# Cross-partition maxima of the activation quantisers: the first over TensorE, GpSimd's last elementwise step given to ScalarE, a rearranged chain of constants, and three output pieces for the first batch

## What is computed

```python
def act_qdq(x, bits=16):
    qmax = 2 ** bits - 1
    mn = jnp.minimum(jnp.min(x), 0.0)          # over the whole tensor
    mx = jnp.maximum(jnp.max(x), 0.0)
    scale = jnp.maximum((mx - mn) / qmax, 1e-12)
    zp = jnp.clip(jnp.round(-mn / scale), 0, qmax)
    q = jnp.clip(jnp.round(x / scale) + zp, 0, qmax)
    return (q - zp) * scale

x = x + xattn(layernorm(x), ctx, Wq, Wk, Wv, Wo)
h = act_qdq(layernorm(x))                       # quantiser 1
up, gate = act_qdq(h @ wu.T), act_qdq(h @ wg.T) # quantisers 3 (up) and 2 (gate)
sig = fixed_qdq(sigmoid(gate), 1 / 65536)
p = act_qdq(gate * sig)                         # quantiser 3 (product)
o = act_qdq(p * up)                             # quantiser 4
x = x + o @ wd.T
```

## Time and profile before

| | |
|---|---|
| executions shown | 863.89, 864.57, 865.39 us |
| profiled execution, own time | 863.88 us |
| its span, first to last instruction | 862.1 us |
| mean granted TensorE clock | 0.966 of full speed |
| busy: TensorE / VectorE / ScalarE / GpSimd | 782.7 / 628.7 / 454.9 / 250.8 us |

### The profile page before, as it was taken

How to read it: one execution, slowest core, us unless ns; L and a number is a source line. 1 busy time by engine, 2 the same in 40 slices (tenths; PEclk the granted TensorE clock), 3 DMA queues, 4 the chain that set the end, 5 groups by cost and what they waited for, 6 DMA issues and landing times. The chain is left out here.

```text
span 862.1 us, 12646 instructions
## 1 busy us (share of the span) xinstructions
PE 782.7 (91%) x4746; PEld 465.3 (54%) x4746; DVE 628.7 (73%) x1141; ACT 454.9 (53%) x965; POOL 250.8 (29%) x382
## 2 busy tenths in 40 slices
PE   8998899999999999999999999997879999600998
PEld 3455466666666666666666666654334444200443
DVE  5873577788768778777788779986475489899741
ACT  5253456656556655566556555555140089495730
POOL 0210314356433466334455443442000012112000
PEclk9999999999999999999999999999989999955999
DMA  9121146756455575456664566997440000000000
GB/s 324 55 81 42 49 122 145 159 127 145 98 131 143 144 171 123 92 141 159 141 151 104 120 137 133 168 169 129 79 81 0 1 1 1 0 1 0 25 37 36
DMA packets 203437, 85.50 MB, mean 99 GB/s; under 512 B 170352, under 2 KB 186736, under 8 KB 203376
## 3 DMA queue, kind: packets, MB, share of 16 engines
q1 hardware_dynamic: 203376, 84.69, 43.1%
HBM read 31.72 MB, written 10.75 MB: 49 GB/s over the span
## 5 line engine op out<-in xcount | busy, mean ns | idle before, releaser
L314 PE MATMUL bank<-arena 128*128 128x256 f16 (+1 forms) x1872 | 261.0, 292 | 5.2 <-DVE arena L729 3.8
L314 PEld LDWEIGHTS bank<-arena 128*128 128x128 f16 x1872 | 182.8, 98 | 87.4 <-DVE arena L729 5.7
L1101 POOL TENSOR_SCALAR arena<-arena,rsum 128x256 f32<-128x256 f32 x256 | 133.7, 522 | 311.3 <-DVE rsum L793 297.3
L729 DVE SCALAR_TENSOR_TENSOR arena<-bank,arena 128x512 f16<-128x512 f32 x168 | 114.7, 688 | 118.1 <-ACT arena L541 117.7
L541 ACT ACTIVATE arena<-bank 128x512 f16<-128x512 f32 x168 | 98.7, 598 | 169.5 <-PE bank L414 93.9
L729 DVE SCALAR_TENSOR_TENSOR arena<-arena 128x512 f16<-128x512 f32 (+3 forms) x195 | 171.2, 889 | 15.3 <-ACT arena L541 14.7
L541 ACT ACTIVATE arena<-arena 128x512 f16<-128x512 f32 (+4 forms) x171 | 135.5, 813 | 61.7 <-POOL arena L1101 19.3
L583 ACT ACTIVATE arena<-bank,nmax 128x256 f32<-128x256 f32 x256 | 117.8, 472 | 60.0 <-DVE nmax L785 58.4
L428 PE MATMUL bank<-arena 128*128 128x512 f16 x512 | 122.4, 382 | 1.7 <-ACT arena L541 1.6
L484 PE MATMUL bank<-arena 128*128 128x512 f16 x528 | 116.7, 385 | 5.8 <-DVE arena L729 5.8
L404 PE MATMUL bank<-arena 128*128 128x256 f16 x768 | 94.3, 273 | 2.8 <-DVE arena L729 2.8
(11 more groups left out here) (87 smaller groups left out, 572.3 us busy)
## 6 DMA issues: line engine op xcount, KB each, us to landing
arena<-in_w_units SPq DMA_DIRECT2D x33, 256.0 KB, 3.6
w_ready<-arena SPq DMA_DIRECT2D x33, 256.0 KB, 3.3
arena<-in_wq SPq DMA_DIRECT2D x32, 256.0 KB, 3.5
arena<-in_wo SPq DMA_DIRECT2D x32, 256.0 KB, 3.6
arena<-in_x SPq DMA_DIRECT2D x1, 2048.0 KB, 15.1
out<-arena SPq DMA_DIRECT2D x8, 256.0 KB, 2.0
arena<-in_wk SPq DMA_DIRECT2D x4, 256.0 KB, 4.0
arena<-in_ctx_t SPq DMA_DIRECT2D x4, 256.0 KB, 4.6
```

The source lines that it names most:

```text
L314: last = nc.tensor.matmul(bank, a(i, c), b(j, c), start=start and c == 0 and n == 0, stop=stop and c == chunks - 1 and n == 2)
L729: return nc.vector.scalar_tensor_tensor(out=dst, in0=src, scalar=scale, in1=part, op0=ALU.mult, op1=ALU.subtract)
L1101: done = nc.gpsimd.tensor_scalar(p_s[:, t % 2, :, hh, :], p_s[:, t % 2, :, hh, :], rsum[:, t % 2, hh:hh + 1], P_SCALE, ALU.mult, ALU.mult)
```

## The change

1. A new path for quantiser 1. After `transpose_x2(B - 1)` TensorE waits for `worst_out` 1 and transposes the 128x2 worst values to 2x128 in PSUM. VectorE takes the maximum of the two rows, spreads it on a 2x2 diagonal, TensorE multiplies that by a 2x128 matrix of ones, which puts both values on all 128 partitions, and VectorE copies them. `all_reduce(1)` is gone, and 14 products on zeros become 12, after this.
2. The last of GpSimd's 11 sigmoid steps (L1174) goes to ScalarE, behind its own L696.
3. The clamp at zero moves out of the chain: `stats` gets one more column, which is zero and takes part in the reductions. The chain to `q_inv` has four steps instead of five, and the one from `q_inv` to `q_set` has one more.
4. Batch 0 of the final rounding goes in three pieces (tiles 0 to 1, 2 to 4, 5 to 10) instead of two.

```diff
-OQ_AT = (0, 5, FT)
+OQ_PIECES = [(0, 0, 2), (0, 2, 5), (0, 5, FT)] + [(b, *span) for b in range(1, B) for span in ((0, 5), (5, FT))]
...
+        ones = f32(178, P)
...
-        stats = small("stats", [P, 5, 2, 2 * FT])
+        stats = small("stats", [P, 5, 2, 2 * FT + 1])
+        x_worst = small("x_worst", [P, 4])
...
             transpose_x2(B - 1)
-            keep_warm(14)
+
+            pe.wait_ge(worst_out, 1)
+            nc.tensor.transpose(banks[SC][0:2, 0:P], worst[:, 0, :], ident[:, :]).then_inc(x_turned, 1)
+            pe.wait_ge(ones_set, 1)
+            pe.wait_ge(x_diag, 1)
+            nc.tensor.matmul(banks[SC + 1][:, 0:2], ones[0:2, :], x_worst[0:2, 1:3], start=True, stop=True).then_inc(x_spread, 1)
+            keep_warm(12)
...
+                    if z == FT - 1:
+                        act.wait_ge(sig_left, FT)
+                        nc.scalar.activation(sig[:, s, :], sig[:, s, :], ACT.Copy, bias=-QMAX, scale=1.0).then_inc(sig_end, 1)
...
             nc.vector.memset(mhalf[:, :], -0.5).then_inc(mhalf_set, 1)
+            nc.vector.memset(stats[:, :, :, :], 0.0).then_inc(stats_set, 1)
+            dve.wait_ge(stats_set, 1)
...
+            nc.vector.memset(ones, 1.0).then_inc(ones_set, 1)
             add_y(STEPS - 1)
...
                 red.then_inc(worst_out, 1)
-                dve.wait_ge(worst_red, number)
-                sets = [(qc[:, q, :], worst_all[:, i, :], worth) for i, (q, _, worth) in enumerate(tensors)]
-                for c, w, worth in sets:
-                    op = nc.vector.tensor_scalar(c[:, 0:2], w, 0.0, worth, ALU.max, ALU.mult)
+                if number == 1:
+                    dve.wait_ge(x_turned, 1)
+                    nc.vector.tensor_reduce(x_worst[0:2, 0:1], banks[SC][0:2, 0:P], AX.X, ALU.max).then_inc(x_top, 1)
+                    dve.wait_ge(x_top, 1)
+                    nc.vector.tensor_scalar(x_worst[0:2, 1:3], ident[0:2, 0:2], x_worst[0:2, 0:1], None, ALU.mult).then_inc(x_diag, 1)
+                    dve.wait_ge(x_spread, 1)
+                    chain(nc.vector.tensor_copy(worst_all[:, 0, :], banks[SC + 1][:, 0:2]))
+                else:
+                    dve.wait_ge(worst_red, number - 1)
+                sets = [(qc[:, q, :], worst_all[:, i, :], worth, -1.0 if q == QP else 1.0) for i, (q, _, worth) in enumerate(tensors)]
+                for c, w, worth, sign in sets:
+                    op = nc.vector.tensor_scalar(c[:, 2:3], w[:, 0:1], w[:, 1:2], 1.0 / QMAX, ALU.add, ALU.mult)
                 chain(op)
-                for c, w, worth in sets:
-                    op = nc.vector.tensor_tensor(c[:, 2:3], c[:, 0:1], c[:, 1:2], ALU.add)
+                for c, w, worth, sign in sets:
+                    op = nc.vector.tensor_scalar(c[:, 3:4], c[:, 2:3], worth, 1e-12, ALU.mult, ALU.max)
                 chain(op)
-                for c, w, worth in sets:
-                    op = nc.vector.tensor_scalar(c[:, 3:4], c[:, 2:3], 1.0 / QMAX, 1e-12, ALU.mult, ALU.max)
-                chain(op)
...
                 op.then_inc(q_inv, 1)
-                for c, w, worth in sets:
-                    op = nc.vector.tensor_scalar(c[:, 5:6], c[:, 1:2], c[:, 4:5], ROUND1, ALU.mult, ALU.add)
+                for c, w, worth, sign in sets:
+                    op = nc.vector.tensor_scalar(c[:, 4:5], c[:, 4:5], worth, -1.0, ALU.mult, ALU.mult)
                 chain(op)
-                for c, w, worth in sets:
-                    op = nc.vector.tensor_scalar(c[:, 5:6], c[:, 5:6], ROUND1, QMAX, ALU.subtract, ALU.min)
+                for c, w, worth, sign in sets:
+                    op = nc.vector.tensor_scalar(c[:, 5:6], w[:, 1:2], c[:, 4:5], ROUND1, ALU.mult, ALU.add)
                 chain(op)
+                for c, w, worth, sign in sets:
+                    op = nc.vector.tensor_scalar(c[:, 7:8], c[:, 5:6], ROUND1, -QMAX, ALU.subtract, ALU.max)
+                chain(op)
...
-            all_reduce(1)
             all_reduce(2)
 
-            for t in range(FT):
+            for t in range(FT - 1):
                 pool.wait_ge(sig_left, t + 1)
```

More of the change, by code:

```diff
@@ L529, in _ @@
                 for t in range(FT):
-                    if t in OQ_AT:
-                        pe.wait_ge(oq_lo, 2 * b + OQ_AT.index(t) + 1)
+                    for i, (batch, first, end) in enumerate(OQ_PIECES):
+                        if batch == b and first == t:
+                            pe.wait_ge(oq_lo, i + 1)
                     for m, (h, r) in enumerate(((0, 0), (0, 1), (1, 0))):
@@ L711, in oq_half @@
             def oq_half(i):
-                b, tiles = i // 2, slice(OQ_AT[i % 2], OQ_AT[i % 2 + 1])
+                b, first, end = OQ_PIECES[i]
                 act.wait_ge(oq_clip, i + 1)
-                hi(oq[:, 0, tiles, b * P:(b + 1) * P], up[:, tiles, b * P:(b + 1) * P], 0.5).then_inc(oq_hi, 1)
+                hi(oq[:, 0, first:end, b * P:(b + 1) * P], up[:, first:end, b * P:(b + 1) * P], 0.5).then_inc(oq_hi, 1)
             act.wait_ge(q_inv, 4)
-            for i in range(2 * B):
-                b, tiles = i // 2, slice(OQ_AT[i % 2], OQ_AT[i % 2 + 1])
-                rounded(up_i[:, tiles, b * P:(b + 1) * P], up[:, tiles, b * P:(b + 1) * P], QO).then_inc(oq_round, 1)
+            for i, (b, first, end) in enumerate(OQ_PIECES):
+                rounded(up_i[:, first:end, b * P:(b + 1) * P], up[:, first:end, b * P:(b + 1) * P], QO).then_inc(oq_round, 1)
                 if i >= 1:
                     oq_half(i - 1)
-            oq_half(2 * B - 1)
+            oq_half(len(OQ_PIECES) - 1)
         @block.vector
@@ L950, in quantisers @@
-                        red = nc.vector.tensor_reduce(worst[:, i, 1:2], stats[:, q, 1, 0:n], AX.X, ALU.max)
+                        nc.vector.tensor_scalar(worst[:, i, 0:1], stats[:, q, 0, 0:1], 0.0, None, ALU.max)
+                        red = nc.vector.tensor_reduce(worst[:, i, 1:2], stats[:, q, 1, 0:n + 1], AX.X, ALU.max)
                     else:
-                        red = nc.vector.tensor_reduce(worst[:, i, :], stats[:, q, :, 0:n], AX.X, ALU.max)
+                        red = nc.vector.tensor_reduce(worst[:, i, :], stats[:, q, :, 0:n + 1], AX.X, ALU.max)
@@ L961, in quantisers @@
                 chain(op)
-                for c, w, worth in sets:
-                    op = nc.vector.tensor_scalar(c[:, 3:4], c[:, 2:3], 1.0 / QMAX, 1e-12, ALU.mult, ALU.max)
-                chain(op)
-                for c, w, worth in sets:
+                for c, w, worth, sign in sets:
                     op = nc.vector.reciprocal(c[:, 4:5], c[:, 3:4])
                 chain(op)
-                for (q, _, _), (c, w, worth) in zip(tensors, sets):
-                    op = nc.vector.tensor_scalar(c[:, 6:7], c[:, 4:5], worth, -1.0 if q == QP else 1.0, ALU.mult, ALU.mult)
+                for c, w, worth, sign in sets:
+                    op = nc.vector.tensor_scalar(c[:, 6:7], c[:, 4:5], worth, sign, ALU.mult, ALU.mult)
@@ L976, in quantisers @@
                 chain(op)
-                for (q, _, _), (c, w, worth) in zip(tensors, sets):
-                    nc.vector.tensor_scalar(c[:, 7:8], c[:, 5:6], -1.0, None, ALU.mult)
+                for c, w, worth, sign in sets:
+                    op = nc.vector.tensor_scalar(c[:, 7:8], c[:, 5:6], ROUND1, -QMAX, ALU.subtract, ALU.max)
+                chain(op)
+                for (q, _, _), (c, w, worth, sign) in zip(tensors, sets):
+                    nc.vector.tensor_scalar(c[:, 5:6], c[:, 7:8], -1.0, None, ALU.mult)
@@ L992, in _ @@
             dve.wait_ge(x2_stat, B)
-            quantisers(1, [(QX, B, 1.0)])
+            dve.wait_ge(ones_set, 1)
+            quantisers(1, [(QX, B, ones[:, 0:1])])
             for i in range(2 * HC + 1):
@@ L1072, in _ @@
             quantisers(4, [(QO, FT, qc[:, QP, 10:11])])
-            for i in range(2 * B + 6):
-                if i < 2 * B:
-                    cols, tiles = slice((i // 2) * P, (i // 2 + 1) * P), slice(OQ_AT[i % 2], OQ_AT[i % 2 + 1])
+            for i in range(len(OQ_PIECES) + 5):
+                if i < len(OQ_PIECES):
+                    b, first, end = OQ_PIECES[i]
+                    cols = slice(b * P, (b + 1) * P)
                     dve.wait_ge(oq_round, i + 1)
[L1077 to L1080, removed]
+                    clip(up[:, first:end, cols], up_i[:, first:end, cols], QO).then_inc(oq_clip, 1)
+                if 1 <= i <= len(OQ_PIECES):
+                    b, first, end = OQ_PIECES[i - 1]
+                    cols = slice(b * P, (b + 1) * P)
                     dve.wait_ge(oq_hi, i)
-                    lo(oq[:, 1, tiles, cols], up[:, tiles, cols], oq[:, 0, tiles, cols], 0.5).then_inc(oq_lo, 1)
-                if i >= 6 and i % 2 == 0:
-                    d = (i - 6) // 2
+                    lo(oq[:, 1, first:end, cols], up[:, first:end, cols], oq[:, 0, first:end, cols], 0.5).then_inc(oq_lo, 1)
+                if i >= 7 and i % 2 == 1:
+                    d = (i - 7) // 2
```

15 lines of the change are left out of this document (8 added, 7 removed).

## The result

| | before | changed |
|---|---|---|
| median of the executions | 864.23 us (863.27 to 865.39, 4) | 857.34 us (856.10 to 857.55, 4) |
| ratio, 95% interval | | 0.9918 (0.9903 to 0.9932) |
| profiled execution's span | 862.1 us | 855.7 us |

What follows compares the result with a forecast made beforehand. Bound by attention, a hole at quantiser 1, TensorE to 747, VectorE and ScalarE with a hole at quantiser 3, then TensorE. Savings 3.35 + 2.4 + 3.1 = 8.85 gave 855.0; half of 1.1 added made 855.5 us, range 853.6 to 858.6.

Steps and rivals of the forecast that it cites:

- the range: Whole kernel: 853.6 to 858.6 us, its lower end from 855.0 less 0.3 and run scatter, its upper taking in three rivals.
- the sum: Whole kernel: 3.35 + 2.4 + 3.1 = 8.85 us saved from the profiled execution, giving 855.0.
- the three gains: First maximum's way 3.35 us, TensorE's clock at the gate and up products 2.4, quantiser 3 3.1.
- The way over TensorE: Quantiser 1, worst values to chain start: five dependent steps of 1.7 us replace 5.11, saving 3.4 us.
- The clock at the first gate product: Start of the 528 gate and up products: TensorE stays at its upper clock, saving 2.4 us.
- rival 1: Ahead of the gate products: the clock falls in the new gap or the zeros before it, costing 2.4: 857.9, chance 0.15.
- Quantiser 3: Third maximum: GpSimd's code change finishes before the worst values, saving 2.98 us; shorter chain saves 0.15; sum 3.1.
- rivals 4 and 5: GpSimd's code loads behind the wait: at second maximum only (863.9, chance 0.02), or after ordinary operations everywhere (875, chance 0.02).
- The tail: Quantiser 4 and output products: zeros hold the start, pieces gain nothing; half of a possible 1.1 us late clock rise counted.
- the new gap: TensorE's remaining pause ahead of the first gate product, behind the 12 zeros: 1.5 us, against 5.78 before.

Runs made afterwards that it cites:

- the two later groups: The changed kernel timed again, unedited, beside other kernels in groups on other chips: 854.30 us (ratio 0.9883), then 855.46 us (ratio 0.9892).
- the third profile: Profile of the unedited changed kernel timed for the third time, in the third group: 855.46 us, ratio 0.9892.
- The profile without zeros: Changed kernel without the 12 products on zeros behind the product with ones at the first maximum: 858.76 us, ratio 0.9928 to the kernel before.
- the kernel with the first maximum alone: Kernel before with only the first maximum moved over TensorE, 12 products on zeros behind it: 858.80 us, ratio 0.9935.
- the kernel with the third alone: Kernel before with only GpSimd's last sigmoid step given to ScalarE, for the third maximum: 862.86 us, ratio 0.9975.

## Why the prediction came out as it did

The time lay within the range and the direction was right; the gain was 6.9 us against 9.1 forecast in the first result, and 10.5 and 9.3 in the two later groups. That the median of all 12 executions, 855.5 us, is the number forecast is partly luck: a start of w1 that the sum didn't have moves the profiles by up to 2.7 us, and in the third profile, where w1 is where it was before, the three gains are 0.3 us more than counted and the late output products 0.7 more. The two parts measured alone add up to 7.2 us (5.6 and 1.6).

- **The way over TensorE**: right in its sum, 1.65 us against 1.7. The product with ones costs 0.53 from the diagonal's end to the copy's start (623.49 + 0.22 = 623.71 to 624.24), where 0.40 was counted, and the transposition 0.36 to its end, where 0.5 was.
- **The clock at the first gate product**: right, 2.6 against 2.4. The reason I gave was half of it. I put it down to the shorter gap. The profile without zeros shows a clock that had fallen before the gap and wasn't brought back, at a price of 2.9 us, and the first profile of the changed kernel one that had fallen at the same place and was. So rival 1, a fall of the clock in or before the new gap, came true in three of eleven profiles without its price of 2.4 us, and by the profile without them the 12 zeros behind the maximum are why.
- **Quantiser 3**: right, 3.06 against 3.1, with the maximum 0.13 us behind `worst`. ScalarE's added step ends at 741.49, 0.18 us before VectorE's multiplication starts, so it costs nothing, but not by much. The sequencer's entries for GpSimd's code stand at 736.8, 7.7 us ahead of w3 (the forecast's "near 741" was in the times of the kernel before, where w3 is 4.6 us later):

```profile
L1191 POOLq MODIFY_POOL_CONFIG  x2: 11/11/11, 736.8 to 736.8; - x2
```

- **GpSimd's load behind the wait** (rivals 4 and 5): excluded by that row and by the second maximum, which costs no stall of TensorE in the 114.1 us. The Trainium skill's figure of about 6 us for the first call to freshly loaded code (GPSIMD Engine Reference, 2.1 "Instruction dispatch") agrees in size with three of the four places where the change of code is waited for: 6.17 and 6.05 us in the kernel before and 6.07 in the kernel with the first maximum alone; the fourth, in the kernel with the third alone, took 7.19. At the third and the fourth maximum of the changed kernel the entries stand 7.7 and 7.8 us ahead of the worst values, so there the load is hidden.
- **The tail**: the mechanism was right (zeros hold the start, the pieces give nothing), the term was mis-sized. I took half of 1.1 us for a late rise of the clock; it was 1.3 us, and 0.9 and 1.2 later. In all three profiles of the changed kernel the start lies at 5.9 to 6.4 us; the 5.03 of the kernel before was the early case, which among the kernels with 16 zeros behind w4 only the one without zeros at the first maximum has again (4.89).
- **What was not in the sum**: the start to w1. I had read the low clock at 602 as evidence on the new gap only, and not asked what it is worth itself and how it varies. It varies by 2.9 us among the profiles, as much as one part of the change.
- **The range**: its lower end, 853.6, doesn't follow from the terms given for it; 855.0 less 0.3 and less 0.7 is 854.0. Nothing measured hangs on it.

So the 2.8 us that the first result lost are low clock in two stretches, 1.5 ahead of w1 and 1.3 behind w4. Shown is that the start to w1 of one and the same kernel is anything from 1.5 us more to 1.2 us less than before, the stretch behind w4 0.9 to 1.3 more, and that all else stays. Not shown is whether a kernel's length biases the instants: in the kernel with the third maximum alone everything behind w3 came earlier and the clock rose no earlier (near 799.9 against 799.4 us), which would take a gain back, but the executions don't separate this from chance.

## What to carry over

Ask of each cross-partition step on GpSimd what ran there before it: the cost of changing code counts from the last ordinary operation, so giving that one operation to another engine can be worth as much as removing the step. When TensorE must wait for constants, put products on zeros right behind the last hand-over: here 12 of them saved 2.9 us of slow products. But put no more than fit before real work is ready: here 16 held up products that could start after 3.8 us, and real products at the lower clock are work done, while zeros are not. And before crediting or blaming an edit for a microsecond or two, compare the stretches that it can't touch.

## What the runs showed that was not expected

Changing GpSimd's code took 6.05 to 7.19 us. With the same program and a pause of about 3 us ahead of it, the granted clock of TensorE near 600 us was not low at all, low for 3.4 us or low for 6.8 us, and the first worst values came between 620.1 and 622.8 accordingly. The median of one and the same kernel moved from 857.3 to 854.3 us between two groups, while the kernel before stayed within 864.2 to 864.9.
